# Scaling by the second norm moved from ahead of the feed-forward layers into the residual's addition behind them

## What is computed

```python
def _encoder_layer(x, Wq, bq, Wk, bk, Wv, bv, Wo, bo, W1, b1, W2, b2, ln1_s, ln1_b, ln2_s, ln2_b):
    h = _layernorm(x, ln1_s, ln1_b)
    ...
    attn = _linear_attention(q, k, v).reshape(b, t, d)
    x = x + (attn @ Wo + bo)
    h = _layernorm(x, ln2_s, ln2_b)
    h = jax.nn.relu(h @ W1 + b1) @ W2 + b2
    return x + h
```

## Time and profile before

| What | Value |
|---|---|
| median of 3 runs | 608.91 us (607.68 to 609.31) |
| profiled execution | 609.01 us |
| its span, first to last instruction | 607.1 us |
| mean granted TensorE clock | 0.997 of full speed |
| TensorE busy, matmuls and transposes | 574.8 us (95% of the span) |
| weight loads, beside them | 539.1 us (89%) |
| VectorE busy | 438.4 us (72%) |
| ScalarE busy | 394.8 us (65%) |
| GpSimd busy | 269.3 us (44%) |

### The profile page before, as it was taken

One profiled execution on the slowest core, in us unless ns is written; L12 is line 12 of the kernel. 1 busy time (PEld: TensorE's weight loads), 2 busy tenths in 40 slices (PEclk: granted clock), 3 DMA queues, 4 the chain that ended last, 5 costly groups with the idle time before them and its releaser, 6 DMA issues.

```text
span 607.1 us, 13106 instructions
## 1 busy us (share of the span) xinstructions
PE 574.8 (95%) x4578; PEld 539.1 (89%) x4578; DVE 438.4 (72%) x1412; ACT 394.8 (65%) x1392; POOL 269.3 (44%) x431
## 2 busy tenths in 40 slices
PE   4889999999899999999999999999999999999977
PEld 3577899998899999998999999997899999998977
DVE  5856577677885777777896777777987665667774
ACT  4667676886575666677585666677675666566641
POOL 5343466664403436654404345646324334446310
PEclk9999999999999999999999999999999999999999
DMA  8500240040000000000000000000000000000000
GB/s 250 172 4 1 80 161 1 23 153 1 20 1 18 2 2 1 2 2 1 2 17 21 0 2 2 2 1 1 1 18 19 2 2 2 1 2 1 2 18 17
DMA packets 10785, 15.58 MB, mean 26 GB/s; under 512 B 969, under 2 KB 8221, under 8 KB 10337
## 3 DMA queue, kind: packets, MB, share of 16 engines
q1 hardware_dynamic: 8368, 11.47, 6.0%
q0 software_dynamic: 720, 2.30, 1.4%
q10 hardware_dynamic: 1632, 0.98, 0.5%
HBM read 12.61 MB, written 2.14 MB: 24 GB/s over the span
## 4 chain that ended last, share of the span: by engine, by line
PE 86%; DVE 5%; POOL 2%; ACT 2%; issue 2%; DMA 1%; SPq 1%; DVEq 0%; POOLq 0%
PE psD L1558 20%; PE psB L1558 19%; PE psA L1558 19%; PE psC L1558 19%; PE psD L1626 1%; PE psB L1626 1%; PE psA L1626 1%; PE psC L1626 1%; DMA wm<-in_wmod 1%; PE psB L1677 1%; PE psC L1677 1%; PE psA L1677 1%; DVE guC L1227 1%; POOL rstdB L817 1%; DVE guD L1101 1%
## 5 line engine op out<-in xcount | busy, mean ns | idle before, releaser
L817 POOL TENSOR_TENSOR rstdD<-msD,neghalf 128x2 f32<-128x2 f32 x36 | 26.2, 727 | 64.1 <-ACT ziD L452 46.8
L817 POOL TENSOR_TENSOR rstdC<-msC,neghalf 128x2 f32<-128x2 f32 x36 | 25.1, 699 | 50.7 <-ACT eqkC L452 50.5
L817 POOL TENSOR_TENSOR rstdA<-msA,neghalf 128x2 f32<-128x2 f32 x36 | 25.6, 712 | 49.3 <-ACT eqkA L452 48.2
L817 POOL TENSOR_TENSOR rstdB<-msB,neghalf 128x2 f32<-128x2 f32 x36 | 25.8, 717 | 36.4 <-ACT eqkB L452 32.6
L452 ACT ACTIVATE eqkA<-xA 128x129 f32<-128x129 f32 x64 | 19.2, 303 | 24.2 <-DVE xA L1148 24.2
L1558 PE MATMUL psC<-w,H 128*128 128x128 f32 x256 | 31.3, 276 | 0.9 <-ACT H L475 0.9
L1558 PE MATMUL psB<-w,H 128*128 128x128 f32 x256 | 31.5, 276 | 0.0
L1558 PE MATMUL psD<-w,H 128*128 128x128 f32 x256 | 31.4, 276 | 0.0
L1558 PE MATMUL psA<-w,H 128*128 128x128 f32 x256 | 31.2, 275 | 0.0
L1558 PEld LDWEIGHTS psC<-w,H 128*128 128x128 f32 x256 | 29.9, 192 | 1.2 <-ACT H L475 1.2
L1558 PEld LDWEIGHTS psB<-w,H 128*128 128x128 f32 x256 | 29.8, 192 | 0.5 <-issue 0.5
(11 more groups left out here) (556 smaller groups left out, 2402.5 us busy)
## 6 DMA issues: line engine op xcount, KB each, us to landing
M<-modulation_rows SPq DMA_DIRECT2D x2, 1280.0 KB, 8.4
M<-modulation_rows SPq DMA_DIRECT2D x1, 2560.0 KB, 8.7
out<-X SPq DMA_DIRECT2D x16, 128.0 KB, 1.9
w<-in_attn_W POOLq DMA_DIRECT2D x1, 1024.0 KB, 8.5
M<-in_attn_W SPq DMA_DIRECT2D x3, 256.0 KB, 4.5
X<-in_attn_x_in ACTq DMA_DIRECT2D x2, 256.0 KB, 3.5
M<-in_attn_W ACTq DMA_DIRECT2D x1, 256.0 KB, 3.6
wo<-in_attn_Wo POOLq DMA_DIRECT2D x1, 256.0 KB, 3.6
```

The costliest lines, as they stand in the source:

```text
L817: pool.tensor_tensor(b.rstd[:, :], b.ms[:, :], neghalf[:, :], ALU.pow).then_inc(b.s_rstd.sem, 1)
```

## The change

The second norm's factor is positive and one per token, so relu(r z) = r relu(z): it may be applied behind the feed-forward layers. Four things are done for that.

The tokens' tile is laid out anew: one constant column, the 128 features, then the root of the mean square and its inverse. The feature that is expressed by the others is now the first one. The transposes of a second norm read 128 columns straight from this tile: the features from the second on, and the root, which takes the place of the 1 that carried the bias (so that the inverse root behind it leaves the bias as it was). `scale` is no longer called for even `n`.

`rstd` of a second norm raises each mean square to +1/2 and to -1/2 in one GpSimd instruction (128x4 values out instead of 128x2). The transposes wait for it, not for VectorE.

`move` behind the feed-forward layers becomes two instructions, one per tile, each with the tile's inverse root as a pointer scalar: PSUM times scalar plus `x`.

`add_bias` of a second norm waits for the transposes (`s_tps`), as these now read `x` itself.

Besides, the written-out orders of all four engines are changed. The cut below has the new functions and those places of the order that the prediction speaks of; the rest are exchanges of the same kind.

```diff
-CONSTS = 4 + 5 * CHAINS
+CONSTS = 6 + 5 * CHAINS
+X_EPS, X_STD, X_RSTD, XW = 0, 1 + D, 2 + D, 3 + D
...
-    base = np.eye(P)
-    base[P - 1, :] = -1
+    base = np.eye(P, k=-1)
+    base[0, :] = -1
...
-            b.xe = [sb(f"x{n}{k}", [P, TILES, D + 1]) for k in range(2)]
+            b.xe = [sb(f"x{n}{k}", [P, TILES, XW]) for k in range(2)]
...
-            return b.xe[i % 2][:, :, 0:D]
+            return b.xe[i % 2][:, :, 1:1 + D]
...
+            pool.memset(halves[:, :, 0:1], 0.5).then_inc(s_const, 1)
+            pool.memset(halves[:, :, 1:2], -0.5).then_inc(s_const, 1)
...
             def rstd(b, i, n):
                 if n <= LAST:
                     pool.wait_ge(b.s_squares.sem, b.s_squares.value(i, n))
+                    if n % 2 == 0:
+                        pool.tensor_tensor(b.xe[i % 2][:, :, X_STD:], b.ms[:, :].unsqueeze(2).to_broadcast([P, TILES, 2]),
+                                           halves[:, :, :], ALU.pow).then_inc(b.s_rstd.sem, 1)
+                        return
                     pool.tensor_tensor(b.rstd[:, :], b.ms[:, :], neghalf[:, :], ALU.pow).then_inc(b.s_rstd.sem, 1)
...
             def add_bias(b, i, n):
-                pool.wait_ge(b.s_normed.sem, b.s_normed.value(i, n))
+                if k == 0:
+                    pool.wait_ge(b.s_normed.sem, b.s_normed.value(i, l + 1))
+                else:
+                    pool.wait_ge(b.s_tps.sem, b.s_tps.value(i, n))
...
             def move(b, i, n):
-                dve.tensor_tensor(x(b, i), b.ps[:, 0, 0:T].rearrange("p (t f) -> p t f", f=D), x(b, i), ALU.add)\
-                    .then_inc(b.s_moved.sem, 1)
+                if n % 2 == 1:
+                    dve.tensor_tensor(x(b, i), b.ps[:, 0, 0:T].rearrange("p (t f) -> p t f", f=D), x(b, i), ALU.add)\
+                        .then_inc(b.s_moved.sem, 1)
+                    return
+                for t in range(TILES):
+                    last = dve.scalar_tensor_tensor(x(b, i)[:, t, :], b.ps[:, 0, t * P:(t + 1) * P],
+                                                    b.xe[i % 2][:, t, X_RSTD:X_RSTD + 1], x(b, i)[:, t, :],
+                                                    ALU.mult, ALU.add)
+                last.then_inc(b.s_moved.sem, 1)
...
             def transposes(b, i, n):
-                norm, src = (n + 1, b.xn) if n < 2 * LAYERS else (LAST, b.z)
-                pe.wait_ge(b.s_normed.sem, b.s_normed.value(i, norm))
+                if n % 2 == 1:
+                    src = b.xe[i % 2][:, :, 2:2 + D]
+                    pe.wait_ge(b.s_rstd.sem, b.s_rstd.value(i, n + 1))
+                else:
+                    src = b.xn if n < 2 * LAYERS else b.z
+                    pe.wait_ge(b.s_normed.sem, b.s_normed.value(i, n // 2 + 1))
```

The order at the end of a step, ScalarE:

```diff
                 squares(D_, i, 8)
-                relu(C, i, 3, 0)
                 tokensT(A, i)
                 transposed(D_, i, 7)
                 tokensT(B, i)
                 relu(D_, i, 3, 0)
                 relu(D_, i, 3, 1)
+                relu(C, i, 3, 0)
+                relu(C, i, 3, 1)
```

and TensorE (the calls of `scale` with even `n` are taken out of VectorE's list; GpSimd's list is the same at this place):

```diff
                 out_project(D_, i, 3)
+                transposes(C, i, 7)
                 out_project2(D_, i, 3)
-                transposes(C, i, 7)
                 logits(A, i)
                 expand(C, i, 3, 0)
                 expand(C, i, 3, 1)
+                logits2(A, i)
                 transposes(D_, i, 7)
-                logits2(A, i)
                 gate(A, i, 0)
+                expand(D_, i, 3, 0)
                 logits(B, i)
-                expand(D_, i, 3, 0)
                 expand(D_, i, 3, 1)
                 logits2(B, i)
```

The order ahead of the loop, TensorE and ScalarE:

```diff
                 project_keys(A, 0, 0)
+                project_queries(A, 0, 0)
                 transposes(B, 0, 0)
-                project_queries(A, 0, 0)
                 sums(A, 0, 0)
                 project_keys(B, 0, 0)
+                attend(A, 0, 0)
                 project_queries(B, 0, 0)
-                attend(A, 0, 0)
                 out_project(A, 0, 0)
...
                 high(0)
+                high(1)
                 squares(B, 0, 1)
-                less_wo_means(0)
                 transposed(A, 0, 0)
                 key_exps(A, 0, 0)
-                high(1)
+                query_exps(A, 0, 0)
                 transposed(B, 0, 0)
```

More of the change, by code:

```diff
@@ L160, in program @@
         neghalf = sb("neghalf", [P, TILES])
+        halves = sb("halves", [P, TILES, 2])
         epsilon = sb("epsilon", [P, TILES])
@@ L535, in _ @@
                 if i == 0:
+                    high(2)
                     high(3)
@@ L609, in _ @@
                 transposed(B, i, 4)
-                if i == 0:
-                    experts_high()
+                squares(D_, i, 4)
                 relu(C, i, 1, 0)
@@ L671, in _ @@
                 squares(D_, i, 7)
+                squares(B, i, 8)
                 key_exps(C, i, 3)
@@ L675, in _ @@
                 query_exps(C, i, 3)
-                squares(B, i, 8)
                 transposed(D_, i, 6)
+                if i + 1 < STEPS:
+                    centre(C, i + 1)
                 squares(A, i, 9)
@@ L1413, in _ @@
                     in_scale(C, i + 1)
+                move(C, i, 5)
                 scale(A, i, 7)
-                move(C, i, 5)
                 divided(D_, i, 2)
@@ L1536, in _ @@
                 gate_up(D_, i, 2)
-                if i + 1 < STEPS:
-                    move(A, i + 1, 1)
                 gate_up(C, i, 2)
@@ L1826, in _ @@
                 transposes(B, i, 2)
+                sums(A, i, 1)
                 expand(C, i, 0, 1)
-                sums(A, i, 1)
                 transposes(D_, i, 1)
@@ L1897, in _ @@
                 expand(A, i, 2, 1)
+                sums(C, i, 2)
                 transposes(B, i, 5)
-                sums(C, i, 2)
                 project_keys(D_, i, 2)
```

377 lines of the change are left out of this document (181 added, 196 removed).

## The result

The changed kernel takes 614.66 us (median of 6 runs, 612.25 to 615.87) against 608.73 for the kernel before. The ratio is 1.0095, with a 95% interval of 1.0076 to 1.0114. That is slower by 0.95%, and the interval leaves no room for no change. The profiled execution took 614.2 us, its span is 612.4.

The account below looks back on a forecast made before the run. TensorE, busy 574.8 of 607.1 us, was taken as the bound, so only its waits count. Four steps at -0.45 us (-1.8) and the start (-0.6) took 609.01 to 606.6 us; range 600.5 to 614.

Parts of the forecast that it names:

- the end of the step: Reordered turn between steps: A's gate 1.0 us earlier, much of it waited out at B's router; -0.55 us per step.
- the start: Work ahead of the loop: new order fills TensorE's waits for A's keys and attention; -0.6 us, 1.5 either way.
- The second rival: GpSimd's in-order queue of powers and biases becomes the wait: 0.35 us per layer, 5.6 in all, 614.6 us; chance 0.22.
- The bias that waits longer: GpSimd's b2 addition waits for the transposes; 0.3 us spare in its queue, so costed at nothing.
- The power that grows: GpSimd's second-norm power of four values: 1.23 us taken, against 0.712 for two; +0.1 us per step with the scaling saved.
- the scaling that goes: 64 VectorE multiplications of 0.419 us ahead of second transposes fall away; 0.48 us saved on that path.
- The split: Addition behind the feed-forward layers becomes two instructions, +0.19 us, offset by relief in VectorE's queue; 0 per step (-0.3 to +0.6).
- The signs: Profile after: half of the scalings gone, VectorE near 424 us; forecast wrong if TensorE waits for GpSimd or first 60 us move over 1.5.

Follow-up runs that it names:

- root_alone: Changed kernel with its orders, but GpSimd's even power writes only the root (two values), a constant standing for the inverse root; 611.06 us, ratio 1.0028.
- before_bias_waits: Kernel before with one edit: second halves' biases wait on GpSimd until TensorE has made the norm's transposes; 612.58 us, ratio 1.0052.
- orders_before: Changed functions, power of four values included, with the kernel before's order of calls on all four engines, even scale calls left out; 610.37 us, ratio 1.0036.
- two_short_powers: Changed kernel with its orders, the power of four values made as two powers of two, the inverse root later; 612.02 us, ratio 1.0061.

## Why the prediction was wrong

It said 606.6 us and faster as the likeliest; it came out at 614.66, 0.66 above the upper end of the range. The direction was wrong. The step that failed is the price of GpSimd's queue, which was taken as covered ("50% of the span and no bound"): +0.1 per step for the longer power and nothing for the waiting bias. Measured, the power's further 0.3 us cost 1.3 per step in the kernel after, and the waiting bias 0.9 per step where it alone was added. Beside it the end of the step came out at +0.3 (mean of the four turns, 24.16 against 23.87) in place of -0.55, and the start at +2.5 in place of -0.6.

The second rival, GpSimd's in-order queue, had the mechanism and nearly the number, at a chance of 0.22. The number is partly luck: the queue and the way to the transposes make some 3 us (1.0095 less the start's share; 3.0 over the last three steps by the markers) where the rival had 5.6, and the start, which the rival did not contain, makes 2.5.

**The bias that waits longer**: "0.3 us are spare, so I cost it at nothing". The run with this wait alone paid 0.9 us per step in the layers. The place that was read, one of A's, does have 0.3 us to spare. The error was to read one place of a queue and let it stand for 64: on the mean GpSimd stood 0.40 longer ahead of each. What was queued behind was taken to be other chains' powers; at the place shown it was their biases and the next step's calls, and where these are missing (step 4) the wait costs 0.34 in place of 0.9. In the kernel after itself, with its own orders, this loss does not show: GpSimd idles 18.2 us ahead of the second biases, less than the 27.6 of the kernel before, and no addition stands for a bias.

**The power that grows** was over-priced and still cost more than expected. The rows gave bounds of 0.71 and 1.23; 1.01 to 1.08 came, 0.16 for each further value. The rule of the Trainium skill, GPSIMD Engine Reference, "Elementwise — side-by-side cycle accounting", would have made it 0.71, an estimate from its cycles per element; the rows after disagree. With the smaller price the way from the squares to the transposes is shorter than before, and by the step's own logic the layers should have gained. Against the kernel before they did not: with the power 0.3 shorter still (root_alone) the layers are 116.37 against 116.29. But there the bias waits too; beside before_bias_waits the scaling that goes is worth its 0.6 per step. Of the shorter way itself little arrives in the orders of before: in orders_before the second norm is ready 1.30 us behind its squares in place of 1.68 (means over the second and third step), and TensorE takes it 1.96 behind them in place of 2.00, so most of it becomes slack. The term was reckoned on one path, and what a longer power does to the calls queued behind it was left out. In the changed orders those 0.3 us are worth 0.75 per step in the layers and 0.54 at the turn.

**The end of the step** (-0.55) was right in direction only for a short power: 23.70 with the root alone against a mean of 23.87. With the long power it is 24.25 in three of four steps. The named place shows it. TensorE's wait for D's second norm is gone from the turn, but C's, moved ahead, now waits 0.78 for its power, and B's router, as named, 0.40. TensorE's timeline of the kernel after:

```profile
422.89 0.44 PE L1635 MATMUL psC<-K,xC 128*128 128x128 f32 x2 [0.78 <-POOL xC L824]
...
430.56 0.61 PE L1563 MATMUL psB<-wr,kpB 128*128 128x8 f32 x4 [0.40 <-ACT xhiB L491]
```

**The split** (0, between -0.3 and +0.6) was right as far as was tried, in the orders of before: some 0.2 per step. The pair took 0.60 to 0.61, as the row from SBUF had it, so 0.19 over the whole addition. **The start** (-0.6, with 1.5 either way) was 2.5 the wrong way. The waits were read as places to be filled; that the changed order could come with a lower granted clock was not considered. **The signs** given ahead did their work: VectorE 426.9 against some 424, half of the scalings gone, waits for GpSimd among TensorE's, and the first 60 us moved by 2.7 (A's first contraction at 44.92 in place of 42.21).

## What to carry to other kernels

Before an engine that is half idle is handed a longer instruction or a later wait, list what stands behind it in its queue, place by place; a spare of 0.3 us at one place is no price for 64. An operation taken off the path gains only as far as its consumer really waits for it (0.48 us off the way here, 0.6 per step of four layers), and a new wait of the old data's next writer (here the bias, because the transposes read `x` itself) belongs to the price of reading in place. Compare such kernels by markers in the loop beside the totals: the layers of a step repeat to 0.05 us where medians of one kernel move by 1.4.

## What was not expected of the hardware

How often TensorE has long half-clock stretches at the start goes with the order of the work there (22 of 45 executions at 0.989 or less against one of 95). One program ran between 607.84 us at 0.994 and 613.95 at 0.985 (root_alone); within the execution that was profiled its steps repeat to hundredths (140.08, 140.07). Another gave its profile at 0.978 with 619.3 us, and 611.1 at 0.996 (two_short_powers). And the same list of instructions has two lengths of its turn within one execution, 23.4 and 24.0 us, and single edits elsewhere change in which steps each comes; why is open.
